# The first pair's orders: third group's w1 low part, fourth group's w2 load, the next pair's last T blocks, 14 warming transposes for 23, C21 in another bank

## The chip, the core and the metric

One core of a Trainium2 chip runs the whole program. The metric is the device time of one execution in microseconds, as the median of several; lower is better. The engines are TensorE (PE; PEld is its weight load), VectorE (DVE), ScalarE (ACT), GpSimd (POOL) and SyncE (SP), which here only issues DMAs.

## What is computed

For each of 16 batches x is 512 tokens by 512 features, float32. Two residual blocks follow one another; the first takes its weights by the batch's language id (one of 10), the second its last 128 output columns by the batch's expert id (one of 8).

```python
# block 1: adapter and layer norm
h = relu(x @ W1[lang] + b1[lang])                    # 512 -> 128
a = x + h @ W2[lang] + b2[lang]                      # 128 -> 512
x = x + layernorm(a) * gamma[lang] + beta[lang]
# block 2: wide layer
h = gelu(x @ W1 + b1)                                # 512 -> 2048
x = x + concat(h @ W2 + b2, h @ We[expert] + be[expert])   # 384 and 128 columns
```

## The kernel before

**Precision.** A float32 product is made of three passes over rounded parts: high by high, high by low, low by high (`three_passes`, L251 to L253). So each operand of block 2 (w1, w2, the activations g and the transposed x) is split into a high part, a rounding copy mostly on ScalarE (`act_..._hi`), and a low part, raw minus high, on VectorE or GpSimd (`dve_..._lo`, `pool_..._lo`).

**Pairs and groups.** The batches are taken two at a time: eight pairs, `first` to `last_pair`. A pair's two batches share the up product x @ W1 by a seven-product scheme (Strassen's, in Winograd's form): the 2048 hidden columns are cut into eight groups k of two 128-column blocks each; per group seven products of 128 by 256 by 512 give the four tiles C11, C12, C22 and C21. Its right operands are B11, B21 (batch 0), B12, B22 (batch 1) and T1 to T4, sums of them; its left operands are blocks of w1 (A11, A12, A22, A21) and sums S1 to S4 of them. The banks up_a, up_b and up_c take the seven products, VectorE adds them up (`dve_sum_q`, `_u2`, `_c12`, `_c22`, `_c21`), ScalarE takes the gelu (`act_g`), VectorE the low part (`dve_g_lo`), and `pe_down` multiplies by w2 into the four banks down[0..3]. Two groups of one batch add up in these banks before VectorE adds them to resid (`dve_down_sum`). The down products of group k stand among the up products of k + 1 and k + 2.

**The first pair.** Only in it the weights come raw from memory: `load_w1_raw`, `load_w2_raw`; GpSimd makes S1 to S4 (`pool_weight_sums`), ScalarE the high part, VectorE the low part (`dve_w1_lo`, `dve_w2_lo`), and SP writes the split weights to memory (`keep_w1`, `keep_w2`), from where later pairs load them. Its group 0 makes the tiles by eight direct products (`first_half`, `pe_first_group`) into the banks FIRST_C, as x becomes ready; each tile's direct products of batch 0 are split in two halves, of B11 and of B21. Ahead of it stands an opening: TensorE transposes x of the first two batches back from xT (`pe_first_x_part`), adds the adapter, and VectorE takes the norm out of the banks. Into this opening TensorE is given transposes of the identity that nobody reads (WARMING, L246, L1577).

**Orders.** There is no scheduler: each engine has one queue, written out by hand. `run` (L1535) calls one step function per engine for each pair i and group k, with m the next pair. The lines of the change stand in these steps and in the opening of each engine at the end of `build`. Every wait is `wait_ge` on a semaphore and holds all that is behind it on its engine. SP's queue (`sp_pair`, L1462) issues nearly all loads and all stores; each has its own waits, and these too hold what is behind. A step of SP in the first pair at k = 3 issued, in this order: keep_w1(3), load_w1_raw(4), the next pair's b1 and vectors for batch 1, its x blocks 0 and 1 and the expert biases, and then keep_w2(2), load_w2_raw(3) and load_experts(3). While the first pair ends (k = 7), the next pair's x is transposed into aux, up_a, up_b and up_c and split, and T1 to T4 are made: T1, T3 and T2 of the first half (c = 0) in the step of k = 7, the second half of T3, T2 and B22 in the step of k = 0 of the next pair.

A bank is free when its readers are done, and that is what `pe_p5` waits for at (first, 1): up_c held B22's first half there, last read by the fifth T block (`dve_t` 5). aux held C21, and `pe_adapter_up` waited for its gelu.

## Time and profile before

| | us |
|---|---|
| runs | 1468.11, 1468.87, 1470.76 |
| median | 1468.87 |
| the profiled execution | 1467.9 |
| its span | 1466.1 |
| TensorE busy | 1449.9 |
| GpSimd busy | 652.1 |
| VectorE busy | 936.5 |
| ScalarE busy | 525.1 |

The span is the time from the first to the last instruction of the profiled execution; the time of a run is a little longer. A busy TensorE can still be at half clock: the granted clock beside a stretch says so.

### The profile page before, as it was taken

To read this page: it belongs to the slowest core of one execution; us is meant where nothing else is said; L and a number is where in the kernel's file an instruction comes from. 1 tells how busy PE (TensorE), PEld (TensorE's weight loads), DVE (VectorE), ACT (ScalarE), POOL (GpSimd) and SP (SyncE) were. 2 spreads that over 40 slices of the span, in tenths; PEclk is the share of its full clock that TensorE was granted. 3 is DMA by queue.
4 is the path that set the end of the run, shared out by engine and by line. 5 is a ranking of instruction groups with operands and counts; after the bars stand their busy time and mean duration, and the time that the engine had idled before them with its cause. 6 is when DMAs were issued, how large, how long until landed. Compare 5 with 4: busy or idle time off the path is not lost.

```text
span 1466.1 us, 19136 instructions
## 1 busy us (share of the span) xinstructions
PE 1449.9 (99%) x6457; PEld 1191.1 (81%) x6457; DVE 936.5 (64%) x1597; ACT 525.1 (36%) x855; POOL 652.1 (44%) x640
## 2 busy tenths in 40 slices
PE   9899999999999999999999999999999999999999
PEld 5787878888888888888888888888888888888887
DVE  6987774866647666576556775566755776554443
ACT  3734363332533234323243322523334332432231
POOL 4895553723454324644147350483413843242101
PEclk9999999999999999999999999999999999999999
DMA  7655558444665536655346644556446464354332
GB/s 219 214 160 197 205 203 299 154 152 158 219 204 171 183 125 222 223 164 196 130 167 223 184 179 156 177 198 205 149 155 229 148 215 157 109 216 149 136 110 86
DMA packets 126616, 261.98 MB, mean 179 GB/s; under 512 B 11572, under 2 KB 83764, under 8 KB 118456
## 3 DMA queue, kind: packets, MB, share of 16 engines
q1 hardware_dynamic: 117300, 157.73, 33.9%
q10 hardware_dynamic: 9220, 103.03, 18.1%
q8 instruction: 52, 0.85, 0.2%
q14 instruction: 44, 0.36, 0.1%
HBM read 222.98 MB, written 37.75 MB: 178 GB/s over the span
## 4 chain that ended last, share of the span: by engine, by line
PE 84%; DVE 1%; issue 0%; ACT 0%; DVEq 0%
PE down L251 14%; PE down L253 14%; PE down L252 14%; PE up_b L251 5%; PE up_b L253 5%; PE up_b L252 5%; PE up_c L252 3%; PE up_c L253 3%; PE up_a L252 3%; PE up_a L251 3%; PE up_c L251 3%; PE up_a L253 3%; PE aux L513 1%; PE aux L252 1%; PE aux L251 1%; PE aux L253 1%
## 5 line engine op out<-in xcount | busy, mean ns | idle before, releaser
L251 PE MATMUL down<-w,g 128*128 128x512 f32 x1024 | 402.4, 393 | 4.2 <-DVE w L1047 3.2
L253 PE MATMUL down<-w,g 128*128 128x512 f32 x1024 | 400.0, 391 | 0.0
L252 PE MATMUL down<-w,g 128*128 128x512 f32 x1024 | 399.7, 390 | 0.0
L1215 POOL TENSOR_TENSOR w<-w_raw,ones 128x256 fp32r<-128x256 f32 x128 | 88.3, 689 | 630.6 <-DMA w_raw<-m_we 630.6
L251 PEld LDWEIGHTS down<-w,g 128*128 128x128 f32 x1024 | 193.0, 189 | 46.4 <-DVE w L1047 4.0
L253 PEld LDWEIGHTS down<-w,g 128*128 128x128 f32 x1024 | 192.9, 188 | 40.6
L252 PEld LDWEIGHTS down<-w,g 128*128 128x128 f32 x1024 | 193.2, 189 | 39.4
L875 DVE TENSOR_TENSOR g<-g_raw,g 128x512 fp32r<-128x512 f32 x256 | 205.9, 821 | 22.1 <-ACT g L660 19.9
L658 ACT ACTIVATE g_raw<-up_a,m_b_sb 128x512 f32<-128x512 f32 x64 | 44.2, 690 | 412.8 <-PE up_a L253 383.5
L870 DVE TENSOR_TENSOR g_raw<-up_b,s 128x512 f32<-128x512 f32 x63 | 43.5, 691 | 225.4 <-PE up_b L253 181.3
L660 ACT CAST g<-g_raw 128x512 fp32r<-128x512 f32 x256 | 159.1, 621 | 8.1
L658 ACT ACTIVATE g_raw<-u,m_b_sb 128x512 f32<-128x512 f32 x63 | 45.6, 724 | 252.5 <-PE down L253 229.7
L251 PE MATMUL up_b<-bo,w 128*128 128x512 f32 x336 | 131.1, 390 | 0.2 <-DVE u L855 0.2
L253 PE MATMUL up_b<-bo,w 128*128 128x512 f32 x336 | 130.8, 389 | 0.0
L252 PE MATMUL up_b<-bo,w 128*128 128x512 f32 x336 | 130.7, 389 | 0.0
L894 DVE TENSOR_TENSOR resid<-down,resid 128x512 f32<-128x512 f32 x128 | 86.9, 691 | 58.9 <-PE down L253 58.9
L1217 POOL TENSOR_TENSOR w<-w_raw,w 128x256 fp32r<-128x256 f32 x128 | 109.6, 857 | 10.1
L658 ACT ACTIVATE g_raw<-g_raw,m_b_sb 128x512 f32<-128x512 f32 x63 | 45.5, 723 | 167.8 <-DVE g_raw L870 167.8
L1208 POOL TENSOR_TENSOR resid<-x,m_bias 128x512 f32<-128x512 f32 x64 | 90.7, 1448 | 0.0
L251 PE MATMUL up_c<-bo,w 128*128 128x512 f32 x224 | 87.6, 391 | 0.0
L252 PE MATMUL up_c<-bo,w 128*128 128x512 f32 x224 | 87.6, 391 | 0.0
L253 PE MATMUL up_c<-bo,w 128*128 128x512 f32 x224 | 87.5, 391 | 0.0
(246 smaller groups left out, 2509.2 us busy)
## 6 DMA issues: line engine op xcount, KB each, us to landing
w<-w_kept ACTq DMA_DIRECT2D x55, 1792.0 KB, 7.9
w<-w_kept SPq DMA_DIRECT2D x56, 768.0 KB, 4.9
w_raw<-m_we SPq DMA_DIRECT2D x128, 128.0 KB, 4.6
out<-resid SPq DMA_DIRECT2D x64, 256.0 KB, 4.9
xTs_raw<-xT SPq DMA_DIRECT2D x56, 256.0 KB, 3.2
xs<-x SPq DMA_DIRECT2D x56, 256.0 KB, 4.9
w_kept<-w SPq DMA_DIRECT2D x8, 1792.0 KB, 7.8
aw_raw<-a_w SPq DMA_DIRECT2D x30, 256.0 KB, 4.6
```

What stands on the lines that cost most here:

```text
L251: eng.matmul(bank, a_hi, b_hi, start=opens, stop=False, skip_group_check=True)
L252: eng.matmul(bank, a_hi, b_lo, start=False, stop=False, skip_group_check=True)
L253: return eng.matmul(bank, a_lo, b_hi, start=False, stop=closes, skip_group_check=True)
L513: last = eng.transpose(bank[:, t * P:(t + 1) * P], x1[:, b, t, c * P:(c + 1) * P], ident[:, :])
L658: eng.activation(values, source, ACT.Gelu, bias=m_b1_sb[:, j:j + 1]).then_inc(act_gelu, 1)
L660: eng.copy(g[:, b, k % 2, h, HI, :], values).then_inc(act_ghi, 1)
L870: eng.tensor_tensor(g_raw[:, 0, k % 2, 1, LO, :], up_b[:, :], s1[:, :], ALU.add).then_inc(dve_c21, 1)
L875: eng.tensor_tensor(g[:, b, k % 2, h, LO, :], g_raw[:, b, k % 2, h, LO, :], raw(g[:, b, k % 2, h, HI, :]), ALU.subtract).then_inc(dve_glo, 1)
L894: eng.tensor_tensor(resid[:, 1, t, :], down[t][:, :], resid[:, 1, t, :], ALU.add).then_inc(dve_out[1], 1)
L1208: eng.tensor_tensor(resid[:, b, t, :], x1[:, b, t, :], m_bias[:, b, :], ALU.add).then_inc(pool_res, 1)
L1215: eng.tensor_tensor(hi, values, ones[:, :, :].to_broadcast([P, 2, PART]), ALU.mult).then_inc(pool_eh[b], 1)
L1217: eng.tensor_tensor(w2[:, k % 2, :, LO, cols], values, raw(hi), ALU.subtract).then_inc(pool_e[b], 1)
```

## The change

**Opening.** WARMING is 12, 2, 0, 0 for 12, 3, 6, 2. FIRST_C puts C21 in up_c for aux, FIRST_B22 puts B22's first half in aux for up_c; the waits of `pe_p5` and `pe_adapter_up` change places with them. TensorE makes the first half of C21 right after pe_first_low of B21, ahead of `pe_first_b12` 2 and 3 and the transposes of B22. ScalarE rounds minus and the second b2 row ahead of `act_first_w_hi`. GpSimd makes the third and fourth root each ahead of one low part of w1, and all four weight sums of group 1 behind its beta sums.

**First pair, groups 0 and 1.** ScalarE takes the next pair's xT 0 and 1 and aw after the gelu of C21, and the gelu of C12 after the first sum s1, where it was ahead of it. VectorE takes `dve_w1_lo(2)` right after g C12 of group 0, ahead of g C22, `dve_w2_lo(1)` and g C11.

**Fourth group.** SP does keep_w2(2), load_w2_raw(3) and load_experts(3), now `first_w2`, at the head of what k = 3 brings for the next pair. For k = 5 and 7 the place is as before.

**End of the first pair.** VectorE takes the last sum, T3 and T2 and B22's low part of the second half in the step of k = 7, ahead of `dve_w2_lo(7)`; they came behind it, and partly in the next step. ScalarE takes T3, T2 and B22's high part ahead of `act_w2_hi(7)`. The other pairs keep their orders.

```diff
--- before.py
+++ after.py
@@ -239,11 +239,11 @@
     FIRST_BANKS = down, (up_b, up_c, aux, down[0])
 
     FIRST_B11, FIRST_B21 = (up_a, down[1]), (down[2], down[1])
-    FIRST_B12, FIRST_B22 = (down[3], up_b), (up_c, down[0])
-
-    FIRST_C = up_a, down[2], down[1], aux
-
-    WARMING = 12, 3, 6, 2
+    FIRST_B12, FIRST_B22 = (down[3], up_b), (aux, down[0])
+
+    FIRST_C = up_a, down[2], down[1], up_c
+
+    WARMING = 12, 2, 0, 0
 
 
 
@@ -353,8 +353,7 @@
         if i is first and k == 1:
             eng.wait_ge(dve_w1, 1)
             wait_first_t(eng, T1)
-
-            eng.wait_ge(dve_t, 5)
+            eng.wait_ge(act_gelu, nth(first, 0, C21))
         if k == 0 and i is not first:
             eng.wait_ge(b_low, i.count(6, 3))
             eng.wait_ge(dve_t, i.count(8, 4))
@@ -440,7 +439,8 @@
         if k == 0:
             eng.wait_ge(aw_split, m.front(4, 2 * b + 1))
             if b == 0 and m is pairs[1]:
-                eng.wait_ge(act_gelu, nth(first, 0, C21))
+
+                eng.wait_ge(dve_t, 5)
             elif b == 0:
                 eng.wait_ge(b_low, m.count(6, 0))
                 eng.wait_ge(dve_t, m.count(8, 0))
@@ -765,6 +765,7 @@
     def act_second_step(eng, i, m):
 
         act_first_sum(eng, i, 1)
+        act_g(eng, i, 0, C12)
         act_g(eng, i, 0, C22)
         act_w2_hi(eng, 0)
         act_w2_hi(eng, 1)
@@ -784,7 +785,7 @@
         if i is first and k == 1:
             act_second_step(eng, i, m)
             return
-        if k == 0 and i is not first:
+        if k == 0 and i is not pairs[1]:
             act_b22_hi(eng, i, 1)
         if k > 0:
             act_g(eng, i, k - 1, C21)
@@ -833,9 +834,12 @@
         act_g(eng, i, k, C22)
         if i is first and k == GROUPS - 1:
             act_t_hi(eng, m, T1, 1)
+            act_t_hi(eng, m, T3, 0)
+            act_t_hi(eng, m, T2, 0)
+            act_b22_hi(eng, m, 1)
         if i is first and k % 2 == 1:
             act_w2_hi(eng, k)
-        if m and k == GROUPS - 1:
+        if m and k == GROUPS - 1 and i is not first:
             act_t_hi(eng, m, T3, 0)
             act_t_hi(eng, m, T2, 0)
 
@@ -1061,10 +1065,10 @@
         dve_xT_lo(eng, m, 0, 2)
         dve_xT_lo(eng, m, 0, 3)
         dve_g_lo(eng, i, 0, C12)
+        dve_w1_lo(eng, 2)
         dve_g_lo(eng, i, 0, C22)
         dve_w2_lo(eng, 1)
         dve_g_lo(eng, i, 1, C11)
-        dve_w1_lo(eng, 2)
 
     def dve_step(eng, i, m, k):
         if i is first and k == 0:
@@ -1079,8 +1083,8 @@
         elif i is not first:
             if before(i) is not first:
                 dve_sum_c21(eng, before(i), GROUPS - 1)
-            dve_t3_t2(eng, i, 1)
-            dve_b_lo(eng, i, B22, 1)
+                dve_t3_t2(eng, i, 1)
+                dve_b_lo(eng, i, B22, 1)
         if k > 0:
             dve_g_lo(eng, i, k - 1, C21)
         elif i is not first:
@@ -1150,12 +1154,14 @@
             dve_t1(eng, m, 1)
             dve_t3_t2(eng, m, 0, up_c)
             dve_b_lo(eng, m, B22, 0, up_c)
+        if i is first and k == GROUPS - 1:
+            dve_sum_c21(eng, i, k)
+            dve_t3_t2(eng, m, 1)
+            dve_b_lo(eng, m, B22, 1)
         if i is first and k % 2 == 1:
             dve_w2_lo(eng, k)
         if k == GROUPS - 1:
-            if i is first:
-                dve_sum_c21(eng, i, k)
-            else:
+            if i is not first:
                 dve_g_lo(eng, i, k, C12)
             dve_g_lo(eng, i, k, C22)
 
@@ -1479,6 +1485,8 @@
                     load_xT_pair(eng, m, 0, 2)
                 if k == 1 or k % 2 == 0 and k > 0:
                     keep_w2(eng, k - 1)
+            if i is first and k == 3:
+                first_w2(eng, k, experts)
             if m:
                 if k == 0:
                     load_aw(eng, m, 0, 1, language_a)
@@ -1502,10 +1510,8 @@
                 store(eng, before(i), 0)
                 load_xT_pair(eng, m, 0, 2)
             if i is first:
-                if k % 2 == 1 and k > 1:
-                    keep_w2(eng, k - 1)
-                    load_w2_raw(eng, k)
-                    load_experts(eng, k, experts)
+                if k % 2 == 1 and k > 3:
+                    first_w2(eng, k, experts)
             elif k % 2 == 1:
                 load_w2(eng, i, k)
                 load_experts(eng, k, experts)
@@ -1526,6 +1532,11 @@
             keep_w2(eng, GROUPS - 1)
             keep_w1(eng, GROUPS)
         return (next_experts, next_language) if m else None
+
+    def first_w2(eng, k, experts):
+        keep_w2(eng, k - 1)
+        load_w2_raw(eng, k)
+        load_experts(eng, k, experts)
 
     def load_xT_pair(eng, m, b, k):
         if m:
@@ -1609,11 +1620,11 @@
             first_half(eng, C11, A11, B11, True, False)
             pe_first_b12(eng, 1)
             pe_first_low(eng, B21, 1, FIRST_B21[1])
+            first_half(eng, C21, A21, B11, True, False)
             pe_first_b12(eng, 2)
             pe_first_b12(eng, 3)
             for c in range(2):
                 pe_transpose(eng, first, 1, 2 + c, FIRST_B22[c])
-            first_half(eng, C21, A21, B11, True, False)
             eng.wait_ge(b_low, 4)
             first_half(eng, C11, A12, B21, False, True)
             first_half(eng, C21, A22, B21, False, True)
@@ -1638,11 +1649,11 @@
             load_first_beta(eng, 1, language)
             load_gamma(eng, first, 1, language)
             act_relu(eng, first, 0)
+            eng.wait_ge(pool_minus, 1)
+            eng.copy(minus[:, :], minus_raw[:, :]).then_inc(act_minus, 1)
+            act_b2_hi(eng, 1)
             act_first_w_hi(eng, 0)
             act_first_w_hi(eng, 1)
-            act_b2_hi(eng, 1)
-            eng.wait_ge(pool_minus, 1)
-            eng.copy(minus[:, :], minus_raw[:, :]).then_inc(act_minus, 1)
             act_relu(eng, first, 1, up_a)
             for t in range(3):
                 act_first_x_copy(eng, t)
@@ -1663,17 +1674,16 @@
                 act_t_hi(eng, first, T1, c)
                 act_b12_copy(eng, first, c, FIRST_B12[c])
             act_w1_hi(eng, 1)
-            for c in range(2):
-                act_xT_hi(eng, pairs[1], 0, c)
-            act_aw_hi(eng, pairs[1], 0, 0)
             eng.wait_ge(in_const, 16)
             act_g(eng, first, 0, C11)
             for c in range(2):
                 act_t_hi(eng, first, T2, c)
             act_g(eng, first, 0, C21)
             for c in range(2):
+                act_xT_hi(eng, pairs[1], 0, c)
+            act_aw_hi(eng, pairs[1], 0, 0)
+            for c in range(2):
                 act_t_hi(eng, first, T3, c)
-            act_g(eng, first, 0, C12)
             run(eng, act_step)
             act_g(eng, last_pair, GROUPS - 1, C21)
 
@@ -1729,15 +1739,14 @@
                               base=0, pattern=[[-1, P]], channel_multiplier=1).then_inc(pool_minus, 1)
             pool_rsqrt(eng, first, 0, 0)
             pool_rsqrt(eng, first, 0, 1)
+            pool_rsqrt(eng, first, 0, 2)
             pool_first_w1_lo(eng, 0)
-            pool_rsqrt(eng, first, 0, 2)
+            pool_rsqrt(eng, first, 0, 3)
             pool_first_w1_lo(eng, 1)
-            pool_rsqrt(eng, first, 0, 3)
-            pool_weight_sums(eng, 1, 0)
             for t in range(TT):
                 pool_first_x_beta(eng, t)
                 pool_rsqrt(eng, first, 1, t)
-            pool_weight_sums(eng, 1, 1)
+            pool_weight_sums(eng, 1)
             run(eng, pool_step)
 
 
```

## Rows read from the trace of the kernel before

**Rows 1.** The page, busy time, share of the span and instructions of each engine.

```profile
PE 1449.9 (99%) x6457; PEld 1191.1 (81%) x6457; DVE 936.5 (64%) x1597; ACT 525.1 (36%) x855; POOL 652.1 (44%) x640
```

**Rows 2.** Waits of TensorE: total us, times, longest us.

```profile
PE up_a L303 <- DVE w L1042: 4.1, 1, 4.1
...
PE down L251 <- DVE w L1047: 3.2, 2, 3.0
...
PE aux L513 <- DVE bo L985: 1.6, 1, 1.6
```

**Rows 3.** Stretches, TensorE: us, busy us (matmuls), granted clock, DMA share, GB/s.

```profile
65.10:72.85 7.75, 3.62 (x9) 0.78 0.56 220
72.85:119.40 46.55, 46.55 (x205) 1.00 0.54 173
119.40:127.67 8.27, 5.26 (x17) 0.79 1.04 411
212.60:219.60 7.00, 4.79 (x17) 0.76 1.05 378
```

**Rows 4.** Timeline of TensorE, opening: start us, us, engine, line, operation.

```profile
6.70 1.39 PE L1578 MATMUL up_c<-ident 128*128 128x128 f32 x6
...
7.93 0.60 PE L481 MATMUL down<-ident,g_raw 128*128 128x128 f32 x4
...
9.02 1.45 PE L470 MATMUL aux<-g_raw,aw_raw 128*128 128x512 f32 x3
```

**Rows 5.** DMA issues of 2.0 to 2.3 and 2.9 to 3.1 us: last number, us to landing.

```profile
g_raw<-xT ACTq DMA_DIRECT2D x2, 256.0 KB, 4.5
...
aw_raw<-a_w SPq DMA_DIRECT2D x1, 256.0 KB, 4.3
```

**Rows 6.** Timeline of TensorE, 34 to 36 us.

```profile
34.39 0.48 PE L530 MATMUL down<-bo,minus 128*128 128x512 f32 x1
...
35.13 0.33 PE L536 MATMUL down<-ident,x 128*128 128x128 f32 x1 [0.26 <-DVE x L966]
```

**Rows 7.** Stretch, ScalarE: us, busy us (instructions), clock, DMA.

```profile
36.15:50.42 14.27, 14.09 (x24) 1.00 0.89 278
```

**Rows 8.** Stretch, all engines, in the order PE, PEld, DVE, ACT, POOL.

```profile
50.56:79.01 28.45, 24.32 (x100) 19.65 (x99) 28.45 (x24) 14.70 (x23) 27.99 (x21) 0.94 0.59 204
```

**Rows 9.** Timeline of VectorE, 66 to 106 us.

```profile
66.90 2.43 DVE L1042 TENSOR_TENSOR w<-w_raw,w 128x1792 fp32r<-128x1792 f32 x1
...
69.85 4.06 DVE L875 TENSOR_TENSOR g<-g_raw,g 128x512 fp32r<-128x512 f32 x3
...
104.93 0.68 DVE L855 TENSOR_TENSOR u<-up_b,s 128x512 f32<-128x512 f32 x1
```

**Rows 10.** VectorE's groups by line, first 50 to 80 us, then 222 to 250.

```profile
L875 DVE TENSOR_TENSOR g<-g_raw,g 128x512 fp32r<-128x512 f32 x8 | 10.6, 1369 | 0.0
...
L875 DVE TENSOR_TENSOR g<-g_raw,g 128x512 fp32r<-128x512 f32 x4 | 2.7, 687 | 0.2 <-ACT g L660 0.2
```

**Rows 11.** Timeline of GpSimd, 59 to 216 us.

```profile
59.06 3.27 POOL L1221 TENSOR_TENSOR bo<-bo_raw,bo 128x512 fp32r<-128x512 f32 x2
...
121.14 1.32 POOL L1217 TENSOR_TENSOR w<-w_raw,w 128x256 fp32r<-128x256 f32 x1
...
208.69 1.31 POOL L1221 TENSOR_TENSOR bo<-t,bo 128x512 fp32r<-128x512 f32 x1 [2.48 <-ACT bo L755]
...
209.95 2.02 POOL L1221 TENSOR_TENSOR bo<-bo_raw,bo 128x512 fp32r<-128x512 f32 x1
...
214.29 1.20 POOL L1217 TENSOR_TENSOR w<-w_raw,w 128x256 fp32r<-128x256 f32 x1
```

**Rows 12.** Timeline of TensorE, 105 to 123 us.

```profile
105.66 0.50 PE L251 MATMUL up_b<-bo,w 128*128 128x512 f32 x1
...
122.56 0.47 PE L251 MATMUL down<-w,g 128*128 128x512 f32 x1 [3.01 <-DVE w L1047]
```

**Rows 13.** Timeline of the SP queue.

```profile
114.23 0.56 SPq L1424 DMA_DIRECT2D w_raw<-m_w  x1
```

## Prediction

> **What bounds the kernel now.** The page first: TensorE is busy for 1449.9 of 1466.1 us [rows 1]. Only its 16.2 us of idle, and the stretches in which it runs at half clock after a stall, can be won. TensorE's own list of waits names them: 4.1 us for VectorE's low part of w1, 3.2 for VectorE's low part of w2, 1.6 for a B block [rows 2]. The table of stretches prices them. From 72.85 to 119.40 it is never idle: 205 matmuls in 46.55 us, 0.227 each [rows 3]. Against that pace:
> - A, 65.10 to 72.85: 8 matmuls (1.8 us) in 7.75 us, loss 5.9. Granted clock 0.78 of full: the stall, then 1.2 GHz for the 3.5 us after it.
> - B, 119.40 to 127.67: 15 matmuls (3.4) in 8.27, loss 4.9, clock 0.79.
> - C, 212.60 to 219.60: four transposes (0.45) and ten matmuls (2.3) in 7.0, loss 4.2, clock 0.76.
> Together 15.0 us, and the opening has some 2 more. All lie in the first pair or at its end; from 220 us on the change touches nothing.
>
> **Opening, warming 23 to 14 transposes.** TensorE never waits from 1.74 us to 9.02 [rows 4]: the warming is in its way if the data is there. The last x block was issued at 2.1 and lands 4.6 later (the median of 4.5 of the last two), 6.7; the adapter weights, issued at 2.98, land after 4.3, at 7.3 [rows 5]. With 12 and 2 warmings the four chunks' transposes follow one another: 4.36, 5.64, 6.5, 7.3, at about 0.85 per four at half clock. pe_first_up then starts at about 7.9 instead of 9.02: 1.1 us earlier. The clock: the transposes take 0.2 us each until the third chunk at 7.93 and 0.11 from there [rows 4], though the granted clock reads 1.0; TensorE is as continuously busy after, so I take the rise at the same time, and no cost. Bounds: 0 (data lands later) to 1.1 gained; the clock's case is a rival.
>
> ScalarE's second b2 row no longer stands behind w1 from memory (it waited to 18.36), so VectorE's statistics run on without its wait of 1.4, and GpSimd's roots go ahead of its w1 low parts. x1 of batch 0 is then ready before TensorE wants it (0.3 idle before 26.47 goes). TensorE reaches the low pass of B21 1.7 us earlier (34.39 to 32.7) [rows 6].
>
> **C21 moved ahead of b12(2) and b12(3).** Six matmuls (1.4 us) fill the time in which these waited, twice, for x1 [rows 6]: idle 34.66 to 36.06 less four transposes of 0.11, 0.95 us. So TensorE starts the second half of C11 2.5 us earlier (38.33 to 35.8). The b12 transposes themselves come only 1.7 - 1.4 + 0.95 = 1.25 earlier, and on them hang the chains of ScalarE and VectorE. ScalarE works without a break from 36.15 to the gelu of C22 at 49.73 [rows 7]; the change only permutes this stretch (xT and aw parts, T3, C12). VectorE's q waits for that gelu and starts at 50.56, now 49.3. The new bank's wait of p5 on the gelu of C21 (about 43.7, p5 at 45.4) and of the adapter on T3 are both met early. Behind p5's wait stands all of TensorE's queue; price 0.
>
> **A, third group's weights.** From 50.56 to 79.01 VectorE is busy all 28.45 us, GpSimd 27.99 [rows 8]. w1_lo(2) goes ahead of g C22 (1.4), w2_lo(1) (1.5) and g C11 (1.75): it starts at about 61.1 instead of 66.90 [rows 9] and ends 63.5. TensorE, 2.5 less 0.8 of waits for w2_lo(0) and the adapter's x blocks, wants it at 63.5: stall A goes. But the three operations passed are due next. pe_down(0, 1) wants w2_lo(1) and g C11, and these end where w1_lo(2) ended, 69.3 less 1.25: 68.1. TensorE is there at 65.35: a new stall of 2.75. Its second half wants g C21 of group 1, before ready at 73.9 [rows 9], now 72.65. So the first 12 matmuls run at half clock inside that time, and pe_down ends at 72.65 + 12 x 0.227 + 0.1 = 75.5 against 72.85 + 5.45 = 78.3 [rows 3]. Gain here 2.8, not 5.9 and more: VectorE's sum is unchanged, only its order.
>
> At one place this rests on how VectorE and GpSimd share SBUF. The same subtraction of g is 0.68 us where GpSimd is idle and 1.37 in this stretch [rows 10]. The Trainium skill (SBUF — State Buffer, Who interferes with whom) has a tensor_tensor with two SBUF inputs and a GpSimd read exclude each other; the trace agrees with its 1.37. By that rule an exchange of order inside a saturated stretch gains nothing by itself, as in my sum.
>
> **Between A and B.** GpSimd's T4 parts start at 59.06 [rows 11], after ScalarE's xT parts; now at 57.15, 1.9 earlier, and its queue runs unbroken to weight_sums(3) at 88.8, ScalarE's w1 and VectorE's w1_lo(3) (90.56), after which VectorE is unbroken to 118.5. So VectorE is 1.9 earlier there. TensorE, 2.75 earlier, meets it at p7 of group 3, which just waited for u2 already (104.93 + 0.68 = 105.61; 105.66) [rows 9, 12]. So 0.85 is given back and 1.9 stays.
>
> **B, fourth group's down weights.** The load is now ahead of load_x, whose wait held SP until 111.5. It was issued at 114.23 [rows 13]; now it waits for keep_w2(2), w2_lo(2) done at 103.8 - 1.9, and the end of pe_down(1, 1): about 102, and lands some 6 us later, 108 (the issued one took 5.7). The experts, whose landing GpSimd awaited until 120.45 with its split ending at 122.46 [rows 11], which is what TensorE's 122.56 [rows 12] stood on, come by 109. Put behind are b1, two vectors and two x blocks: due at 118 or later, landing by 116. Next late is VectorE: busy to 118.5 - 1.9 = 116.6, then w2_lo(3) (1.04): TensorE goes on at 117.65, 0.15 after it wants to. Start 122.56 to 117.65 is 4.9, and the half clock behind the stall (15 matmuls in 5.1 instead of 3.4) goes: 1.7. **Gained at 127: 6.6**, the 1.9 in it.
>
> **C, T blocks ahead.** TensorE waited for B22's low part (214.3) and then for the experts' split on GpSimd (214.29 + 1.20 = 215.5; TensorE 215.60) [rows 11]. In the time of before: VectorE does sum_c21 at 209.7, T3, T2 and B22's low to 212.2, then w2_lo(7) to 213.2. The first wait goes. The second is GpSimd's. Its low part of T3 took 2.02 where T1's before it, beside VectorE's reads of PSUM, took 1.31 [rows 11]; VectorE's work there now reads PSUM, so I take 1.3 for T3 and T2, and the split is done at 214.1. Start gains 1.5 (bounds 0, if the lows stay slow, to 2.6, if nothing waits). Of the half clock, 1.45 us, I take half: the idle left is 1.1, between waits of 0.3 that left the clock alone [rows 6] and 1.8 + 0.8, which did not. **C: 2.2**, bounds 0 to 4.0.
>
> **Sum.** 6.6 + 2.2 = 8.8. The profiled execution took 1467.9 (span 1466.1 and 1.8 around it), 1.0 below the median of 1468.87. 1467.9 - 8.8 = 1459.1, as a median 1460.1.
>
> **Rivals.**
> 1. GpSimd and VectorE get in each other's way less after the shift, and A, B and C go whole: 15.0 less some 2 for the new stall at pe_down(0, 1): 13, 1456.0. For it: contention is half of VectorE's time there. Against: nothing takes work from either engine.
> 2. Only B is gained: VectorE starts q no earlier (a link of the opening is kept by memory, as w1's landing at 18.36), A only moves, C ends on GpSimd as before. 122.56 to 119.55 and 1.7: 4.7, 1464.2. For it: each is one link.
> 3. The load at B does not come earlier (SP is held by kept_w2 or the store). Then 1.9 + 2.2 = 4.1 at most, and with 2's links under 3: about 1466.5.
> 4. Slower: the clock does not rise at 7.9 without the eight last warmings, and TensorE, with its small idles in the opening, stays at 1.2 GHz from 7.9 to 22.65: the 13.6 us of matmuls from 9.02 double. +13.6 - 1.1, less the 7.7 of B and C: +4.8, 1473.7. It decides from 8.8 us of half-clock cost on. For it: 0.2 us a transpose says that the early clock is low. Against: TensorE has no gap before 7.9. [...]
>
> **Chances.** Forecast 0.60, rival 1 0.13, rival 2 0.18, rival 3 0.06, rival 4 0.03. A difference of 0.2% (2.9 us) is what a measurement can tell. Faster 0.93 (forecast, 1, 2 and a third of 3), same 0.04, slower 0.03. Range 1456.4 to 1464.4: A to B between 4.7 and 7.5, C between 0 and 4, and the two near rivals' edges; outside stay 3, 4 and part of 1.
>
> **What would show it.** First adapter matmul near 7.9; q near 49.3; no wait at p1 of group 2 but 2 to 3 us before pe_down(0, 1); pe_down(0, 3) near 117.7 without a wait over 0.5; one idle of about 1 us before pe_down(0, 7) at C. Wrong if q is at 50.5, if w2's load of group 3 is issued after 105, or if a stretch behind 220 us differs.

## The result and the profile after

| | before | after |
|---|---|---|
| median of 20 runs each, us | 1468.51 (1463.75 to 1474.67) | 1466.06 (1464.31 to 1467.82) |
| ratio, 95% interval | 1 | 0.9979 [0.9971, 0.9987] |
| span of the profiled execution | 1466.1 | 1464.3 |

The change makes the kernel faster by 2.5 us between the medians, 3.1 by the ratio (1.9 to 4.3 by its interval) and 1.8 in the span, not by 8.8. Ratios here and below leave out slow executions; there was one, of a_warm, 2077.56 us at a granted clock of 0.655.

Names that come up again and again: p1 to p7 are TensorE's seven products of a group; pe_down(b, k) is the down product of batch b and group k, 24 matmuls in two halves of 12, the first waiting for the split of w2 and of the expert, and each half for the low part of its own tile of g; q and u2 are two of VectorE's sums of a group. In the fences of timelines the columns are start us, us, engine, line, operation, and in brackets the idle before and what ended it. Lines have moved: VectorE's low part of g is L879 (it was L875), of w2 L1051 (L1047), of w1 L1046 (L1042); GpSimd's expert split is L1221 and L1223 (L1215, L1217). TensorE's waits after, against [rows 2]:

```profile
PE down L251 <- POOL w L1223: 2.6, 1, 2.6
PE down L251 <- DVE g L879: 2.3, 2, 2.1
PE down L251 <- issue: 1.9, 1, 1.9
...
PE up_a L303 <- DVE w L1046: 0.5, 2, 0.3
...
PE down L251 <- DVE w L1051: 0.3, 1, 0.3
```

Of the three old waits the one for a B block is gone and the other two are down to 0.3 at most each time, and three new ones stand in their places: 2.6 at A, 2.1 at B, 1.9 at C. TensorE's timeline has where:

```profile
7.53 3.70 PE L470 MATMUL aux<-g_raw,aw_raw 128*128 128x512 f32 x8
...
33.12 0.48 PE L530 MATMUL down<-bo,minus 128*128 128x512 f32 x1
...
64.38 0.73 PE L303 MATMUL up_a<-bo,w 128*128 128x512 f32 x2 [0.28 <-DVE w L1046]
69.14 0.47 PE L251 MATMUL down<-w,g 128*128 128x512 f32 x1 [2.65 <-POOL w L1223]
...
104.89 0.50 PE L251 MATMUL up_b<-bo,w 128*128 128x512 f32 x1 [0.67 <-DVE u L859]
...
119.13 0.50 PE L251 MATMUL down<-w,g 128*128 128x512 f32 x1 [0.33 <-DVE w L1051]
124.20 0.50 PE L251 MATMUL down<-w,g 128*128 128x512 f32 x1 [2.06 <-DVE g L879]
...
213.65 0.64 PE L251 MATMUL down<-w,g 128*128 128x512 f32 x1 [1.85 <-issue]
```

How far TensorE is ahead of before, step by step: 1.27 us at the low pass of B21 [rows 6], 0.82 at VectorE's q (50.56 to 49.74), 2.0 behind A, 0.77 at p7 of group 3 [rows 12], 3.43 at the start of pe_down(0, 3), 1.07 at its end (129.73 to 128.66), 1.39 at 207.9, 1.93 at p6 of pair 1 (222.72 to 220.79), against 1.8 in the span. So the story is in two places: A's gain is handed back by 105, and B's 3.43 shrinks to 1.07 within 10 us.

VectorE and GpSimd at B, after:

```profile
118.99 0.68 DVE L874 TENSOR_TENSOR g_raw<-up_b,s 128x512 f32<-128x512 f32 x1
119.59 4.55 DVE L879 TENSOR_TENSOR g<-g_raw,g 128x512 fp32r<-128x512 f32 x3
```

```profile
118.58 1.64 POOL L1182 TENSOR_TENSOR x<-xs,vecs 128x512 f32<-128x512 f32 x1
120.30 1.62 POOL L1184 TENSOR_TENSOR xs<-xs,vecs 128x512 f32<-128x512 f32 x1
121.89 1.71 POOL L1182 TENSOR_TENSOR x<-xs,vecs 128x512 f32<-128x512 f32 x1
123.67 1.61 POOL L1184 TENSOR_TENSOR xs<-xs,vecs 128x512 f32<-128x512 f32 x1
```

The same two engines there before:

```profile
122.40 1.28 DVE L875 TENSOR_TENSOR g<-g_raw,g 128x512 fp32r<-128x512 f32 x2
123.92 0.69 DVE L875 TENSOR_TENSOR g<-g_raw,g 128x512 fp32r<-128x512 f32 x1 [0.24 <-ACT g L660]
```

```profile
121.14 1.32 POOL L1217 TENSOR_TENSOR w<-w_raw,w 128x256 fp32r<-128x256 f32 x1
122.42 1.66 POOL L1201 TENSOR_TENSOR rstd<-var_eps,minus_half 128x1 f32<-128x1 f32 x2
124.05 1.70 POOL L1176 TENSOR_TENSOR x<-xs,vecs 128x512 f32<-128x512 f32 x1
```

Three low parts of g took 1.28 + 0.69 = 1.97 us while GpSimd made roots of one column; now they take 4.55, 1.52 each, beside four bias sums of 128 by 512. Before, the late experts held GpSimd's queue until 122.42, and so kept the bias sums out of VectorE's way. With the experts early, the queue behind them slid forward by 5.5 us, under the very operation that the second half of pe_down(0, 3) waits for. The stretches (us, busy us (matmuls), granted clock, DMA share, GB/s), before and then after:

```profile
118.00:131.00 13.00, 9.99 (x37) 0.87 0.87 335
```

```profile
118.00:131.00 13.00, 10.62 (x39) 0.87 0.63 203
205.00:222.00 17.00, 15.15 (x67) 0.90 0.62 221
```

The half clock is there in this execution as before (0.87). And C, GpSimd after, against [rows 11]:

```profile
207.32 1.30 POOL L1227 TENSOR_TENSOR bo<-t,bo 128x512 fp32r<-128x512 f32 x1 [2.48 <-ACT bo L755]
208.57 1.31 POOL L1227 TENSOR_TENSOR bo<-bo_raw,bo 128x512 fp32r<-128x512 f32 x1
209.83 1.30 POOL L1227 TENSOR_TENSOR bo<-h_raw,bo 128x512 fp32r<-128x512 f32 x1
211.08 1.33 POOL L1221 TENSOR_TENSOR w<-w_raw,ones 128x256 fp32r<-128x256 f32 x1
212.49 1.05 POOL L1223 TENSOR_TENSOR w<-w_raw,w 128x256 fp32r<-128x256 f32 x1
```

The low parts of T3 and T2 take 1.3 each, as forecast (they took 2.02 and 1.72), but the split itself now takes 1.33 + 1.05, where it took 0.61 + 1.20, and VectorE's low parts of w2 and g (210.76 to 214.1) now lie beside it; no run takes them away, so that they are the cause is read from the timelines only. From the first low part to the split's end: 6.80 us before, 6.22 after. So C's start gained 0.58 by itself.

### The profile page after: what moved, and what is told of

The parts are those of the page before. It is cut to its first block, busy times and chain, and to the rows that moved or that the text cites. A ratio compares the mean times of both kernels' runs of the same rounds, so it can differ in the third digit from the quotient of the medians.

```text
span 1464.3 us, 19118 instructions
## 1 busy us (share of the span) xinstructions
PE 1449.0 (99%) x6448; PEld 1188.7 (81%) x6448; DVE 942.4 (64%) x1597; ACT 525.3 (36%) x855; POOL 654.3 (45%) x640
## 4 chain that ended last, share of the span: by engine, by line
PE 90%; POOL 4%; DVE 3%; issue 2%; ACT 0%; DMA 0%; SPq 0%; ACTq 0%; DVEq 0%; POOLq 0%
PE down L251 15%; PE down L252 15%; PE down L253 15%; PE up_b L251 5%; PE up_b L253 5%; PE up_b L252 5%; PE up_c L253 4%; PE up_c L251 4%; PE up_c L252 4%; PE up_a L251 3%; PE up_a L252 3%; PE up_a L253 3%; POOL resid L1214 1%; DVE g L879 1%; PE aux L513 1%
## 5 line engine op out<-in xcount | busy, mean ns | idle before, releaser
L1221 POOL TENSOR_TENSOR w<-w_raw,ones 128x256 fp32r<-128x256 f32 x128 | 90.8, 709 | 619.9 <-DMA w_raw<-m_we 619.9
L879 DVE TENSOR_TENSOR g<-g_raw,g 128x512 fp32r<-128x512 f32 x256 | 208.4, 831 | 21.9 <-ACT g L660 19.5
L1223 POOL TENSOR_TENSOR w<-w_raw,w 128x256 fp32r<-128x256 f32 x128 | 106.9, 835 | 10.0
```

The lines of the kernel that those rows point to most:

```text
L879: eng.tensor_tensor(g[:, b, k % 2, h, LO, :], g_raw[:, b, k % 2, h, LO, :], raw(g[:, b, k % 2, h, HI, :]), ALU.subtract).then_inc(dve_glo, 1)
L1221: eng.tensor_tensor(hi, values, ones[:, :, :].to_broadcast([P, 2, PART]), ALU.mult).then_inc(pool_eh[b], 1)
L1223: eng.tensor_tensor(w2[:, k % 2, :, LO, cols], values, raw(hi), ALU.subtract).then_inc(pool_e[b], 1)
```

## The experiments

Each was timed against the kernel before on the same chip. The medians come from different chips, so the ratios are what can be compared between rows. "p6" is the start of p6 of pair 1 in the one profiled execution; it sums up the first pair, but with the chance of that execution in it. Nine kernels share the new opening, and VectorE's q of group 1 starts between 49.17 and 49.74 in them; and a stall at B or C costs 1.6 us of half clock in one execution and none in another (see the end). So a part is read below at its own place, between two matmuls around it, before p6 is used.

| run | median us | ratio [95%] | span | p6 |
|---|---|---|---|---|
| before (profile) | 1468.51 | 1 | 1466.1 | 222.72 |
| after | 1466.06 | 0.9979 [0.9971, 0.9987] | 1464.3 | 220.79 |
| x1_hold | 1464.12 | 0.9961 [0.9947, 0.9975] | 1462.8 | 216.80 |
| x2_exp7 | 1465.05 | 0.9971 [0.9958, 0.9983] | 1461.4 | 215.53 |
| x3_both | 1463.06 | 0.9954 [0.9940, 0.9967] | 1460.5 | 213.70 |
| p_b | 1467.23 | 0.9987 [0.9978, 0.9997] | 1464.7 | 219.28 |
| p_c | 1468.14 | 0.9995 [0.9983, 1.0007] | 1468.4 | 222.66 |
| a_noa | 1465.23 | 0.9972 [0.9960, 0.9985] | 1464.0 | 218.11 |
| a_warm | 1467.49 | 0.9991 [0.9979, 1.0004] | 1465.2 | 221.38 |
| a_nob_r | 1466.85 | 0.9992 [0.9979, 1.0004] | 1468.2 | 221.34 |
| x5_store_late | 1460.49 | 0.9945 [0.9929, 0.9961] | 1458.4 | 213.82 |
| x6_exp1_r | 1461.04 | 0.9945 [0.9929, 0.9960] | 1461.2 | 213.82 |
| x5_no_c_r | 1460.73 | 0.9948 [0.9933, 0.9962] | 1458.6 | 215.07 |

**x1_hold: the bias sums held back.** GpSimd's step of k = 4 in the first pair:

```diff
+            pool_expert(eng, i, 1, 3)
+            eng.wait_ge(dve_glo, i.count(4 * GROUPS, 4 * 4))
             pool_biases(eng, m, 1, 0)
             pool_biases(eng, m, 1, 1)
-        elif k > 1:
+        elif k > 1 and k != 4:
             pool_expert(eng, i, 1, k - 1)
```

> The changed kernel with one edit in GpSimd's queue at group 4: the split of the fourth group's expert weights goes first, and the next pair's two bias sums of batch 1 wait until VectorE has made the low part of g C21 of group 3. Theory (VectorE and GpSimd hinder each other): in the changed kernel these sums lay beside VectorE's three low parts of g, which took 4.55 us instead of the 2.0 of before; held back, the three take under 3 us, the second half of pe_down(0, 3) starts at about 121.9 instead of 124.20, the half clock behind that stall goes, and everything from there is 3.5 to 4 us earlier: about 1462.3. Rival (VectorE simply started too late, or ScalarE's gelu of C21 is what g waits for): the three still take over 4 us or start late, the stall stays over 1.5 us, time unchanged within 0.5.

```profile
119.22 2.43 DVE L879 TENSOR_TENSOR g<-g_raw,g 128x512 fp32r<-128x512 f32 x3
```

```profile
118.00:131.00 13.00, 12.70 (x56) 1.00 0.62 196
```

The three low parts take 2.43 instead of 4.55, the stall is gone, 56 matmuls fit in the 13 us where 39 did, and p6 comes 4.0 us earlier, as expected. The ratio falls from 0.9979 to 0.9961, 2.6 us, though the two intervals just overlap. The edit also brings the split of expert (1, 3) forward, to 118.21 to 120.50, partly beside the low parts, and they stay short all the same. That it was the bias sums that stretched g is shown, and with it why B gave so little.

**x2_exp7: the experts' split of group 7 ahead of the T parts.** GpSimd, first pair:

```diff
                 if n == 0:
                     pool_first_w1_lo(eng, 3)
+                    pool_expert(eng, i, 0, k)
...
-        if k % 2 == 1 and k > 1:
+        if k % 2 == 1 and 1 < k < GROUPS - 1:
```

> The changed kernel with GpSimd's split of group 7's expert weights of batch 0 moved ahead of its T low parts, into its idle time of 204.8 to 207.3. Theory (at the pair's end TensorE waited for that split, ending at 213.54, and for nothing else): pe_down(0, 7) starts at about 212.0, when w2_lo(7) is done, instead of 213.65, and without the half clock behind it (1.5 us): 1.7 or, with the clock, 3.2 us less, 1462.9 to 1464.4. Rival (the T low parts, now 1.4 to 2.4 us later, become the wait at p6 or p7 of the next pair): time unchanged or up to 1 us more.

```profile
209.94 0.50 PE L251 MATMUL down<-w,g 128*128 128x512 f32 x1 [0.20 <-DVE w L1051]
...
245.84 0.47 PE L251 MATMUL down<-w,g 128*128 128x512 f32 x1 [1.59 <-issue]
```

C's stall is GpSimd's split and nothing else: 1.85 became 0.20, and with the half clock behind it the stretch from the next pair's p1 (207.91 in after) to p6 falls from 12.88 us to 9.67. Of the 5.3 us that p6 is earlier, 3.2 are this; most of the rest is B's stall, which stood as before (2.06) but without a half clock behind it in this execution. A new wait of 1.59 appears 36 us later, and the ratio moves only from 0.9979 to 0.9971, less than expected and inside the intervals.

**x3_both: the two edits together**, nothing else.

> Both edits at once, in two places 90 us apart. Theory: they add up, 3.7 + 3.2 = 6.9 us less than the changed kernel, about 1459.2. Rival (what is won at group 4 is taken back by an engine that runs through, as GpSimd or a load, before 200 us): no more than the second edit alone gives.

The first pair is 7.1 us shorter than after's, but the ratio says only 3.7 us (0.9979 to 0.9954) where 6.9 were expected: the new wait grows to 2.21 at 244.63. GpSimd's timeline names it:

```profile
242.64 0.97 POOL L1221 TENSOR_TENSOR w<-w_raw,ones 128x256 fp32r<-128x256 f32 x1 [23.92 <-DMA w_raw<-m_we]
```

```profile
225.00:245.00 20.00, 17.79 (x79) 1.00 1.04 374
```

The experts of pair 1 have not landed; the DMA engines are full (share 1.04) in the stretch that stores the first pair and reads the next one's x. TensorE got there earlier, the transfer did not.

**p_b: before, with only the fourth group's loads moved.** Its edit to the kernel before is the change's own, in SP's step:

```diff
+            if i is first and k == 3:
+                first_w2(eng, k, experts)
...
-                if k % 2 == 1 and k > 1:
+                if k % 2 == 1 and k > 3:
```

> The kernel before with the fourth group's loads ahead in SP's queue and nothing else of the change. The prediction's step B in full would be 4.9 us less (1463.6). Theory now: TensorE starts pe_down(0, 3) at about 119.7 instead of 122.56, when VectorE's w2 low part is done, but its second half then waits for g C21, since GpSimd's bias sums start at once and lie beside VectorE: the three low parts take over 4 us, and the end of pe_down(0, 3) moves from 129.7 by less than 1 us; time within 1 us of before. Rival (the load was not on time or DMA was full): pe_down(0, 3) starts after 121.

```profile
120.30 0.50 PE L251 MATMUL down<-w,g 128*128 128x512 f32 x1 [0.34 <-DVE w L1047]
125.37 0.50 PE L251 MATMUL down<-w,g 128*128 128x512 f32 x1 [2.02 <-DVE g L875]
```

The new stall comes with this part alone: start 2.26 earlier, 2.02 given back five us later, g's low parts again 4.55 (at 120.76). The end of pe_down(0, 3) is 1.49 earlier and not less than 1 as expected, because here neither this stall nor C's had a half clock behind it (granted clock 1.00 in both stretches); that is also why p6 is 3.4 earlier. Ratio 0.9987, 1.9 us.

**p_c: before, with only the T blocks moved.** VectorE's step (ScalarE's is the change's too):

```diff
+        if i is first and k == GROUPS - 1:
+            dve_sum_c21(eng, i, k)
+            dve_t3_t2(eng, m, 1)
+            dve_b_lo(eng, m, B22, 1)
         if i is first and k % 2 == 1:
             dve_w2_lo(eng, k)
```

> The kernel before with only the last T blocks ahead (step C). The prediction's step C would be 2.2 us less. Theory now: of TensorE's two waits the first goes and the second grows, since GpSimd's split of the experts is what ends both; GpSimd's T3 part takes 1.3 instead of 2.0, so pe_down(0, 7) starts 0.5 to 0.7 us earlier than 215.60, and the clock is as before: 0.6 us less. Rival (the first wait was a loss of its own): over 1.5 us less.

One wait of 1.85 ends at 215.53, where before had two that ended at 215.60, and p6 is the same to 0.06. But this execution reached the place late: the next pair's p1 starts at 209.80, in before at 209.30. From there to pe_down(0, 7) it is 5.73 us for 6.30. So C alone is worth 0.57 at its place, as expected, and the same 5.73 or 5.74 stands in every kernel with C and the late split; the ratio, 0.9995, cannot show so little.

**a_noa: after, with A undone.**

```diff
         dve_g_lo(eng, i, 0, C12)
-        dve_w1_lo(eng, 2)
         dve_g_lo(eng, i, 0, C22)
         dve_w2_lo(eng, 1)
         dve_g_lo(eng, i, 1, C11)
+        dve_w1_lo(eng, 2)
```

> The changed kernel with w1's low part of group 2 back behind g C22, w2's low part and g C11 on VectorE (step A undone). Theory (A only changes the order inside a stretch in which VectorE runs through, and what follows at p7 of group 3 hangs on VectorE and GpSimd, not on TensorE): the stall of 4 us at p1 of group 2 is back, the end of pe_down(0, 1) moves from 76.3 to about 77.5, but VectorE's u2 of group 3 stays at 104.2 and from there nothing changes: time within 0.5 us of the changed kernel. Rival (the forecast's view that 2.8 us are won at A and 1.9 kept): everything from group 3 is over 1 us later.

```profile
67.91 1.07 PE L303 MATMUL up_a<-bo,w 128*128 128x512 f32 x2 [4.40 <-DVE w L1046]
```

```profile
118.00:131.00 13.00, 10.66 (x46) 1.00 0.56 179
```

The stall of 4.4 is back, and nothing is lost: from q to u2 of group 3 VectorE takes 54.30 us (49.17 to 103.47), with A it took 54.42 (49.74 to 104.16). The ratio is 0.9972, the same as after's within the intervals. That p6 is 2.7 earlier is not A's: 0.6 of it is there at q already, and 1.6 is a half clock that did not come at B. The second row will be wanted below.

**a_warm: after, with all the warmings.**

```diff
-    WARMING = 12, 2, 0, 0
+    WARMING = 12, 3, 6, 2
```

> The changed kernel with the warming transposes as before, 12, 3, 6 and 2. Theory (the nine transposes stood in the way; the opening's chain is led by TensorE): the adapter's first matmul is back from 7.53 to about 9.0, but 0.5 us of it is what ScalarE's relu costs in the changed kernel, so q of group 1 moves from 49.74 by 0.5 to 1.0 and the whole by the same. Rival (with fewer warmings the clock rises later, and the gain is paid back): q not later than 49.9.

First adapter matmul 8.38 (7.53), q 50.09 (49.74), p6 +0.59; the ratio goes back from 0.9979 to 0.9991. q is later than in all nine executions without the nine transposes (49.17 to 49.74, mean 49.53). So leaving them out is worth about 0.6 us at q and 1.8 by the ratios, whose intervals overlap; 1.8 is more than the first pair shows.

**x5_store_late: x3_both, with the store of the first pair's batch 0 behind the loads of w2 and of the experts.** SP's queue, pair 1, k = 0:

```diff
-                store(eng, before(i), 0)
+                if i is not pairs[1]:
+                    store(eng, before(i), 0)
                 load_xT_pair(eng, m, 0, 2)
...
                 load_experts(eng, k, experts)
+                if i is pairs[1] and k == 0:
+                    store(eng, before(i), 0)
```

> The kernel with both edits on GpSimd (the held bias sums and the early expert split), and in SP's queue at the start of pair 1 the store of the first pair's batch 0 (1 MB) moved behind the loads of w2 and of the experts. Theory (the 2.2 us stall at 244.6 that came up with both edits is a landing: DMA is busy without a break from 225 to 245, and the expert weights land behind the stores; TensorE is there 7 us earlier than in the kernel before): the split on GpSimd starts at 240 instead of 242.6, the stall is under 0.5, the time 1.5 to 2.2 less than with both edits alone, 1461. Rival (the landing is set by w1's and w2's reload, not by the store): the stall stays above 1.5.

```profile
239.68 0.62 POOL L1221 TENSOR_TENSOR w<-w_raw,ones 128x256 fp32r<-128x256 f32 x1 [20.84 <-DMA w_raw<-m_we]
```

```profile
225.00:245.00 20.00, 20.00 (x90) 1.00 1.04 370
```

The same DMA share, but the experts are there 3 us earlier (242.64 to 239.68) and TensorE is busy all 20 us. SP issues their loads from 228.01, in x3_both from 230.59. How much of the 3 us is the order's, one execution does not tell: in the two runs below with the same order of SP this wait of GpSimd ends at 241.90, and at 236.15 with a second one to 239.75. The ratio, 0.9945 against 0.9954, is inside the intervals too. This version beats both kernels: 5.5 thousandths under before, 8.1 us, with an interval that ends below after's.

**a_nob_r: after, with B undone.**

```diff
-            if i is first and k == 3:
-                first_w2(eng, k, experts)
...
-                if k % 2 == 1 and k > 3:
+                if k % 2 == 1 and k > 1:
```

> The changed kernel with B undone: first_w2(3) stands again where the next pair's loads have gone out, so the load of w2 raw of group 3 is issued near 114 us. What is read: the start of pe_down(0, 3) near 121.8 (122.56 less the 0.8 carried), with a wait of about 3 us for the experts' split, no stall in front of its second half (the bias sums of GpSimd end the low parts' company). Theory (B's stall was only exchanged for another, so B is worth 0.3 to 1.3 us in this kernel as it was alone): median ratio 0.998 to 0.999 against the kernel before, 0.3 to 1.3 us above the changed kernel. Rival (the carried 0.8 is all that the start of pe_down(0, 3) gives, B itself costs by its low parts): ratio as the changed kernel or below, 0.997 to 0.998.

```profile
122.94 0.77 PE L251 MATMUL down<-w,g 128*128 128x512 f32 x1 [4.26 <-issue]
```

```profile
118.00:131.00 13.00, 8.74 (x27) 0.74 0.80 310
```

The start was expected near 121.8, with the 0.8 carried; it is 122.94, later than before's 122.56, and the clock falls lower (0.74). GpSimd waits for the experts to 120.65 (120.45 before), although SP issued their loads 0.92 earlier (114.06 for 114.98). So without B what the opening wins is swallowed here, and B is what lets it pass. The second half does not wait: g's low parts take 2.42. Ratio 0.9992, against 0.9979: 1.9 us for B, more than the theory's 1.3, with intervals that overlap.

**x6_exp1_r: x5_store_late, with GpSimd's split of expert (0, 1) ahead.**

```diff
+            pool_expert(eng, i, 0, 1)
             pool_expert(eng, i, 1, 0)
             pool_aw_lo(eng, m, 0, 1)
-            pool_expert(eng, i, 0, 1)
```

> x5_store_late with GpSimd's split of expert (0, 1) taken ahead of expert (1, 0) and of the adapter's low part in group 1: the split that ends the new stall at pe_down(0, 1) is done 2 us earlier. Theory (what TensorE gains in this stretch is given back at p7 of group 3, since VectorE is the bound from 50 to 105 us): the stall of 2.65 at 69 shrinks to about 1.9 (g C11's low part ends it), u2 of group 3 stays at 104.0 within 0.2, and the median stays at that of x5_store_late within 0.5. Rival (the stall at A is a loss of its own, above all by the half clock behind it): the median falls by 0.7 to 2.3 us.

```profile
67.92 0.47 PE L251 MATMUL down<-w,g 128*128 128x512 f32 x1 [1.53 <-DVE g L879]
72.90 0.50 PE L251 MATMUL down<-w,g 128*128 128x512 f32 x1 [2.00 <-DVE g L879]
```

The split no longer ends the stall at 69, but the wait moves to the second half: 2.65 became 1.53 + 2.00. u2 of group 3 is at 103.95 (103.99) and the ratio is that of x5_store_late, although a wait of 1.31 at 243.86, for the experts of pair 1, is back in this execution. So the orders tried only choose which matmul waits, and u2 of group 3 stays. But VectorE is not, as both expectations had it, the bound of the whole stretch. It stands idle ahead of w1's low part of group 3; before, and then after:

```profile
90.56 2.75 DVE L1042 TENSOR_TENSOR w<-w_raw,w 128x1792 fp32r<-128x1792 f32 x1 [3.17 <-ACT w L759]
```

```profile
89.80 2.74 DVE L1046 TENSOR_TENSOR w<-w_raw,w 128x1792 fp32r<-128x1792 f32 x1 [4.42 <-ACT w L759]
```

ScalarE waits there in turn for GpSimd's last weight sum, which ends at 88.80 before and at 88.03 after. GpSimd's queue has no gap from q to this sum, so it is the bound up to here, and A, which changes only VectorE's order, cannot move it: VectorE comes to its wait 2.0 us earlier, waits 1.25 longer, and is left with 0.76.

**x5_no_c_r: x5_store_late, with C undone**, p_c's edit taken back:

```diff
-        if i is first and k == GROUPS - 1:
-            dve_sum_c21(eng, i, k)
-            dve_t3_t2(eng, m, 1)
-            dve_b_lo(eng, m, B22, 1)
```

> x5_store_late with C undone: VectorE and ScalarE take the next pair's last T blocks behind w2 of group 7 and partly in the next step again, GpSimd's split of the experts of group 7 stays early. Theory (C gave nothing only because GpSimd's split set the end of the stall; with the split early the T order does count): a wait of 1 to 2 us for the low part of B22 (near 209 to 210) and one for w2_lo(7) come back, p6 of pair 1 is 1 to 2.5 us later than 213.82, median ratio 0.9955 to 0.9965. Rival (the T order never mattered): p6 of pair 1 within 0.3 of 213.8, ratio 0.9945.

```profile
209.10 0.66 PE L513 MATMUL aux<-ident,x 128*128 128x128 f32 x4 [1.64 <-DVE bo L986]
```

With the split early, the T order does set the end: this wait is back and p6 is 1.25 later. But span and ratio stay within 0.2 us and 0.3 thousandths of x5_store_late, since its later pairs were that much shorter in the profiled execution. The theory holds at the place; its worth for the whole time is under what these runs tell.

## Why the forecast was wrong, step by step

The mechanism of B was half right, the sum was not. The step that failed is this one: "TensorE goes on at 117.65, 0.15 after it wants to. Start 122.56 to 117.65 is 4.9, and the half clock behind the stall (15 matmuls in 5.1 instead of 3.4) goes: 1.7. Gained at 127: 6.6". Measured there, at the end of pe_down(0, 3): 1.07. The 5.5 us between:

- **2.06, the second half's stall.** The forecast stopped at the start of pe_down(0, 3), and let g's low parts keep the 2.0 us that they had beside GpSimd's one-column roots; the bias sums, moved under them, made it 4.55. Shown by x1_hold and p_b. The forecast had quoted the very rule for A (the Trainium skill, SBUF — State Buffer, Who interferes with whom: a VectorE instruction with two SBUF inputs contends with a GpSimd one that reads SBUF), and its [rows 10] had the price, 1.37 against 0.69 each. The trace agrees at B too, 1.52 against 0.66. It was not asked again where GpSimd's queue moved.
- **1.7, the half clock.** A stall remained, and the clock fell behind it in this execution; in three of five with this stall it did not, so this part is chance as much as error.
- **1.13 + 0.34, the start.** The carried shift was 0.77, not 1.9. "Now at 57.15, 1.9 earlier" took GpSimd's T4 parts to hang on ScalarE alone. GpSimd's own queue is unbroken from 49.66 before and 48.77 after, so T4 starts at 57.97, 1.09 earlier, and VectorE's w1_lo(2), now beside the split of an expert, made that 2.40 us from 1.07. By group 3 only q's 0.8 was left: GpSimd's last weight sum ends 0.77 earlier, and all that follows hangs on it. The other 0.34 is again a neighbour: with the experts early, GpSimd's split of them (110.12 to 112.33) lies beside two VectorE operations, and w2_lo(3) behind these starts at 118.12. After, and then before:

```profile
109.49 2.24 DVE L977 SCALAR_TENSOR_TENSOR x<-x,rstd,xs 128x512 f32<-128x512 f32 x2
```

```profile
110.25 1.88 DVE L973 SCALAR_TENSOR_TENSOR x<-x,rstd,xs 128x512 f32<-128x512 f32 x2
```

They take 2.24 in p_b too and 1.89 in a_nob_r, where B is undone.

- The rest, 0.3, is spread.

**Opening.** Right in kind: the first adapter matmul came at 7.53, better than the 7.9. The 0.4 on top is luck: the forecast let the rate double at 7.9, and in the two executions of this opening in which it doubled about that late (x3_both, x5_store_late) the matmul came at 7.87 and 7.88. And it bought nothing in this execution: of 1.49 there, 1.0 was left behind the relu, 1.27 at 34 us and 0.82 at q (forecast 1.7 and 1.25). The step from 34 us to q, 0.45 for C21's place, was forecast right; all that is missing at q, 0.43, is missing at 34 us already, and the relu took 0.5. ScalarE's timeline of the opening:

```profile
8.41 0.62 ACT L691 CAST bo<-bo_raw 64x512 fp32r<-64x512 f32 x1 [4.11 <-DMA bo_raw<-a_b]
8.54 0.83 ACTq L1378 DMA_DIRECT2D bo_raw<-a_b  x2
...
11.66 0.69 ACT L677 ACTIVATE h_raw<-aux,a_b_sb 128x512 f32<-128x512 f32 x1 [2.63 <-PE aux L470]
```

It waits for a bias row to 8.41 and then issues DMAs to 11.5, while the adapter matmuls are done at 11.23 (7.53 + 3.70); TensorE waits 0.5 for the relu. In x2_exp7 the adapter matmuls begin at 7.03, in x3_both at 7.87, and the relu at 11.58 and 11.51: all that x2_exp7 was ahead was lost at ScalarE. The landing of the bias row has a part in it: in a_noa and x5_no_c_r the wait for it ended at 7.34 and 7.33 and not at 8.41, and the relu began at 11.10 and 10.93, right behind the matmuls.

**A.** Right in its outline: the stall at p1 fell from 4.1 to 0.3, a new one came at pe_down(0, 1), and what was won was given back at p7. That it measured 2.65 for a forecast 2.75 is luck. TensorE came to it at 66.49 and not at 65.35, and it ended at 69.14 and not at 68.1, on an engine that the forecast did not name there:

```profile
67.99 1.05 POOL L1223 TENSOR_TENSOR w<-w_raw,w 128x256 fp32r<-128x256 f32 x1
```

That is GpSimd's split of expert (0, 1). With it moved ahead, in x6_exp1_r, pe_down(0, 1) starts at 67.92, on VectorE's low part of g as forecast. Behind A TensorE was 2.0 ahead, not 2.8. a_noa goes further than the forecast did: that A is worth anything here these runs don't show.

**C.** Start gain forecast 1.5, half clock 0.7, measured 0.58 and none, 0.54 at p6. The term that was mis-sized is again a duration beside a moved neighbour: the split's 1.81, which became 2.38. And the forecast counted half of the half clock as won, since an idle of 1.1 would be left; it was 1.85, and the clock fell.

**The sum.** 8.8 - 5.5 (B) - 1.7 (C) + 0.3 (small waits between 130 and 208) leaves 1.9, and the span says 1.8. Rival 2 named the kind of the failure (links of the opening kept, A only moved, C ends on GpSimd) but gave B its 4.7 whole, 1464.2; less than that was won. Rival 3 had about the time, 1466.5, but not the cause: the load was issued at 103.70, as forecast. Rival 4's case, the early clock, did not come: in all nine executions with 14 warmings the transposes run at the double rate by 7.9, as in before. With three more edits (the bias sums, the split of group 7, the store) the kernel reaches 1460.49. That this is close to the forecast of 1460.1 does not bear out the sum: the edits take away costs that the forecast had kept, as C's idle, beside the one that it had overlooked.

## What to carry to other kernels

When a transfer or an operation is made earlier, everything behind it on its queue comes earlier too: list what slides, under whom, and price the waiting engine's operations by rows with that neighbour busy. Follow the gain through to the last half of the block that it feeds, not to its first matmul. And look for the engine that has no gap (here GpSimd from 49 to 88 us): an exchange of order on another engine only chooses who waits.

## What was not expected of the hardware

**The same stall costs a half clock in one execution and not in the next.** After and a_noa have nearly the same stall at the same place (2.06 and 2.01) and the same busy time between 118 and 131 us (10.62 and 10.66), but 39 matmuls at a granted clock of 0.87 in one, 46 at 1.00 in the other: 7 matmuls, 1.6 us. Behind the 1.85 at C, the clock of 205 to 222 is 0.90 in after, a_noa, a_warm, p_c and x1_hold, and 1.00 in a_nob_r. Of five executions with this stall of 2.0 at B the clock fell in two (after, a_warm) and not in three (p_b, x2_exp7, a_noa): the last 12 matmuls of pe_down(0, 3) take 4.46 and 4.09, or 2.86 to 2.89. What decides it these runs don't show. So a profile of one execution can move by 1.6 us for each such stall, and the forecast's terms for it were a chance and not a price.

**The early clock too.** The kernels with 23 warmings are not alike in it. In before the six warmings at 6.70 took 1.39 us and the rate doubled at about 7.9 [rows 4]; in p_b, with the same opening, it had doubled before 5.4:

```profile
5.34 0.60 PE L481 MATMUL down<-ident,g_raw 128*128 128x128 f32 x4
...
7.53 3.60 PE L470 MATMUL aux<-g_raw,aw_raw 128*128 128x512 f32 x8
```

Its first adapter matmul comes at 7.53 for 9.02, yet its q is no earlier (50.97), so a faster start was worth nothing there. All of TensorE's work up to the doubling is transposes, in before as here.

**The last seven pairs wander.** From p6 of pair 1 to the last matmul it is 1239.7 us in before, 1239.8 in after, 1242.4 in x1_hold and 1239.9 in x5_no_c_r, under the same orders or nearly; a whole pair takes 177.7 or 178.5 without a wait that a view would show. That is why a part of 1 us is read here at its own place in the first pair, and the whole time only from ratios.
